# Second slots of a mixture-of-experts layer: units of two experts by half the sequences, in one block with the first slots

## The reference, cut to what matters

```python
GROUP = 64; E1, S1, E2 = (8, 16, 4)
logits1 = einsum('bGgd,esd->bGges', xg, phi)
disp1 = softmax(logits1, axis=2)
comb1 = softmax(logits1.reshape(b, G, g, E1 * S1), -1)
slots = einsum('bGgd,bGges->bGesd', xg, disp1)            # first slots
yn = _l2norm(slots) * scale * gamma2
means = yn.reshape(b, G, E1, m, ns, d).mean(axis=4)       # m = 4 means per expert
se2 = einsum('bGkmd,kdf->bGkmf', means, w_slot2)          # second slots
se2 = _l2norm(se2.reshape(..., E2, d)...) * scale
logits2 = einsum('bGksd,bGkemd->bGksem', yn, se2)
disp2 = softmax(logits2, axis=3)
comb2 = softmax(logits2 ..., -1)
slots2 = einsum('bGksd,bGksem->bGkemd', yn, disp2)        # dispatch: inputs of the experts
u = einsum('bGkemd,kedh->bGkemh', slots2, w1) + b1        # 32 small experts
...
```

## Time and profile before

| what | value |
|---|---|
| median of 3 runs | 555.93 us |
| lowest, highest | 555.88, 558.68 us |
| profiled execution, whole time | 558.41 us |
| its span, first to last instruction | 556.6 us |
| mean granted clock of TensorE | 0.997 |
| PE busy | 529.9 us (95%) |
| DVE busy | 314.0 us (56%) |
| ACT busy | 251.7 us (45%) |
| POOL busy | 103.1 us (19%) |

### The profile page before, as it was taken

One profiled execution on the slowest core, in us unless ns is written; L12 is line 12 of the kernel. 1 busy time (PEld: TensorE's weight loads), 2 busy tenths in 40 slices (PEclk: granted clock), 3 DMA queues, 4 the chain that ended last, 5 costly groups with the idle time before them and its releaser, 6 DMA issues. The chain is left out here.

```text
span 556.6 us, 13660 instructions
## 1 busy us (share of the span) xinstructions
PE 529.9 (95%) x5485; PEld 438.6 (79%) x5485; DVE 314.0 (56%) x727; ACT 251.7 (45%) x807; POOL 103.1 (19%) x189
## 2 busy tenths in 40 slices
PE   6999999999999999999898999999989999999996
PEld 5888888865566566666777856988879999999985
DVE  2348679666877776663268745376634444444433
ACT  1234343456656656644377558456732222222210
POOL 6380000011044034321217700000100000000000
PEclk9999999999999999999999999999999999999998
DMA  6090000000000000000380032000059999999643
GB/s 242 16 317 3 2 0 2 1 1 1 1 2 2 2 1 1 1 2 1 112 358 2 2 126 88 2 1 2 1 194 409 276 347 369 363 309 332 164 58 114
DMA packets 20724, 58.82 MB, mean 106 GB/s; under 512 B 3043, under 2 KB 9797, under 8 KB 20549
## 3 DMA queue, kind: packets, MB, share of 16 engines
q1 hardware_dynamic: 14756, 49.47, 24.8%
q0 software_dynamic: 1056, 4.33, 4.1%
q10 hardware_dynamic: 4848, 4.13, 2.7%
HBM read 53.21 MB, written 4.33 MB: 103 GB/s over the span
## 5 line engine op out<-in xcount | busy, mean ns | idle before, releaser
L2030 PE MATMUL banks<-slots_t,w 64*128 64x128 f32 x1344 | 80.7, 272 | 1.1 <-PEq L1654 1.1
L1135 DVE TENSOR_REDUCE qk<-banks 128x4 f32<-128x1024 f32 x48 | 58.8, 1225 | 39.5 <-PE banks L598 39.5
L2030 PEld LDWEIGHTS banks<-slots_t,w 64*128 64x128 f32 x1344 | 79.1, 188 | 1.5 <-issue 1.3
L598 PE MATMUL banks<-qk_t 16*128 16x256 f32 x384 | 54.4, 400 | 2.6 <-DVE qk L1135 2.4
L605 PE MATMUL banks<-qk_t 17*128 17x256 f32 x384 | 54.4, 400 | 0.0
L598 PEld LDWEIGHTS banks<-qk_t 16*128 16x128 f32 x384 | 33.2, 184 | 20.3 <-issue 13.8
L2133 DVE TENSOR_REDUCE tokens<-banks 128x192 f32<-128x384 f32 x32 | 17.8, 557 | 47.3 <-PE banks L2061 47.3
L99 PE MATMUL banks<-ident 128*128 128x128 f32 x342 | 43.4, 278 | 0.0
L99 PEld LDWEIGHTS banks<-ident 128*128 128x128 f32 x342 | 40.3, 192 | 2.7 <-issue 2.6
L914 ACT ACTIVATE wk_t<-banks 128x512 f32<-128x512 f32 x48 | 26.1, 595 | 32.8 <-PE banks L605 32.8
L338 POOL TENSOR_TENSOR qk<-qk,att_rms 128x384 f32<-128x384 f32 x14 | 11.4, 837 | 150.6 <-ACT att_rms L886 150.6
(11 more groups left out here) (243 smaller groups left out, 1114.8 us busy)
## 6 DMA issues: line engine op xcount, KB each, us to landing
w<-in_w SPq DMA_DIRECT2D x28, 768.0 KB, 11.9
w<-in_w2e SPq DMA_DIRECT2D x24, 384.0 KB, 12.4
w_slot<-in_w_slot SPq DMA_DIRECT2D x8, 576.0 KB, 4.2
yn_t<-in_w SPq DMA_DIRECT2D x4, 768.0 KB, 11.0
yn_t<-in_w2e SPq DMA_DIRECT2D x8, 384.0 KB, 14.1
rows_scratch<-tokens ACTq DMA_DIRECT2D x28, 96.0 KB, 7.1
yn_all<-rows_scratch POOLq DMA_DIRECT2D x7, 384.0 KB, 9.5
out<-h SPq DMA_DIRECT2D x8, 192.0 KB, 1.9
```

What stands on the lines that cost most here:

```text
L598: last_best = nc.tensor.matmul(g.ps[MAXES[hh]][:, half * SEQ:(half + 1) * SEQ], g.qk_t[bn_ % 2][row:row + HDIM, bq, 0, half * P:(half + 1) ...
L1135: nc.vector.tensor_reduce(to, flat(MAXES[0], MAXES[1] + 1).rearrange("p (h t n) -> p h t n", h=2, n=SEQ), AX.X, ALU.max, negate=True).then ...
L2030: return nc.tensor.matmul(bank[:, j * P:(j + 1) * P], g.w1[n % BUFS][rows, first + j * P:first + (j + 1) * P], x, start=start, stop=stop, ...
```

## The change

The two functions become one, `slots_and_dispatch`, with one block. Its parts:

1. The second slots are made in eight units `u` instead of eight experts. A unit is two experts for half the sequences (16 groups, 64 columns of means). Units 0 to 3 are for sequences 0 to 3, units 4 to 7 for sequences 4 to 7. `make_se2(u)` has eight matmuls in place of four: each is 64 columns wide and goes to the lower or upper 64 partitions of a bank. `parts` yields four copies each for DVE and ACT, of half the size, in place of two.
2. `make_se2(0)` stands ahead of the last `make_slots`, where twelve `keep_busy` matmuls stood. `make_se2(1)` follows `turn_last`. The DVE list has `norm_se2(0)` and `norm_se2(1)` among the seven `sum_last` reductions, and on ACT `keep_last` follows the third unit.
3. The logits of sequence 0 and their softmax stand among the last two units. Of the 87 `keep_busy` matmuls in the two functions 23 are left: 3 at the start as before, 16 before `turn_last`, 4 in the last sequence.
4. In the dispatch `make_weights` is split in two, with `turn_disp` between the halves.
5. All eight weight tiles are loaded at the start of the block: three in `w_slot2`, four in the tiles of `w1`, one in the region that later holds `slots2_t`, which also holds the temporaries of the first slots. `w1` of the first four experts is loaded when all units are made.
6. Since two blocks with their semaphores stand where three were, the mixer's 53 semaphores (`early_semaphore`) are cleared by SP at the end of the mixer's own block, after the last projection, and no longer in the next block.

```diff
@@ mixer_and_attention, SP
+            sp.wait_ge(S["projected"], BATCH)
+            sp.wait_ge(S["mixed_kept"], BATCH)
+            sp.wait_ge(S["divided"], BATCH)
+            sp.wait_ge(S["tokens_made"], BATCH - 2)
+            g.clear_early(sp)
@@ slots_and_dispatch
+        weights2 = [*g.w_slot2, *(tile[:, 0:3 * E2 * DIM // 2] for tile in g.w1), carve([P, 3 * E2 * DIM // 2])]
+        MADE = (2, 4, 2, 4, 0, 2, 4, 0)
@@ PE: a unit
+                for b in range(2):
+                    for x in range(2):
+                        nc.tensor.matmul(g.ps[MADE[u] + b][x * REST:(x + 1) * REST, 0:COLS], means(x, slice(0, P), 0),
+                                         weights2[first + x][:, b * COLS:(b + 1) * COLS], start=True, stop=False,
+                                         skip_group_check=True)
+                for x in range(2):
+                    for b in range(2):
+                        rows = slice(b * REST, (b + 1) * REST)
+                        last = nc.tensor.matmul(g.ps[MADE[u] + b][x * REST:(x + 1) * REST, 0:COLS], means(x, rows, 1),
+                                                weights2[first + x][rows, 2 * COLS:3 * COLS], start=False, stop=True,
+                                                skip_group_check=True)
@@ PE: its list from the last pass of first slots on
-            pe.wait_ge(S["comb_kept"], BATCH - 1)
-            keep_busy(nc, g, 2, 12)
+            make_se2(0)
             make_slots(BATCH - 1)
             turn_yn(BATCH - 2)
             turn_comb(BATCH - 1)
-            keep_busy(nc, g, 2, 12)
+            pe.wait_ge(F["rest_kept"], BATCH - 2)
+            keep_busy(nc, g, 1, 16)
             turn_last(BATCH - 1)
-            keep_busy(nc, g, 2, 18)
+            make_se2(1)
+            for u in range(2, UNITS):
+                make_se2(u)
+                turn_se2(u - 2)
+            make_logits(0)
+            turn_se2(UNITS - 2)
+            turn_logits(0)
+            turn_se2(UNITS - 1)
+            for n in range(1, BATCH):
+                make_logits(n)
+                make_weights(n - 1, range(0, PAIRS))
+                turn_disp(n - 1)
+                make_weights(n - 1, range(PAIRS, GPS))
+                turn_logits(n)
+                make_inputs(n - 1)
@@ ACT
+            for u in range(UNITS):
+                root_se2(u)
+                if u >= 2:
+                    keep_se2(u - 2)
+                if u == 2:
+                    keep_last(BATCH - 1)
+            row_exp(0)
+            keep_se2(UNITS - 2)
+            col_exp(0)
+            keep_se2(UNITS - 1)
@@ DVE
             norm_slots(BATCH - 1)
-            sum_last(BATCH - 1)
+            norm_se2(0)
+            sum_last(BATCH - 1, slice(0, 4))
+            norm_se2(1)
+            sum_last(BATCH - 1, slice(4, 7))
+            keep_se2(0)
+            for u in range(2, UNITS - 1):
+                norm_se2(u)
+                keep_se2(u - 1)
+            mask(0)
+            norm_se2(UNITS - 1)
+            keep_se2(UNITS - 2)
+            col_max(0)
+            invert_row(0)
+            keep_se2(UNITS - 1)
+            dispatch(0)
@@ SP
+            for k in range(E1):
+                sp.dma_start(weights2[k][:, :], g.d["w_slot2"][k]).then_inc(weights2_loaded[k // 2], 16)
+            for n in range(EARLY):
+                load_output(sp, g, n)
+            g.clear_before(sp)
+            sp.wait_ge(S["made"], UNITS)
+            for n in range(EARLY):
+                load_hidden(sp, g, n)
...
```

More of the change, by code:

```diff
@@ L7 @@
+import math
 from contextlib import ExitStack
@@ new lines, in logits @@
+            def logits(n):
+                pe.wait_ge(F["kept"], n + 1)
+                if n >= 2:
+                    pe.wait_ge(F["comb_exped"], TPS * (n - 1))
+                    pe.wait_ge(F["comb_kept"], n - 1)
+                if n >= 3:
+                    pe.wait_ge(F["rest_kept"], n - 2)
+                for part in range(2):
+                    for to_slots in (True, False):
+                        for t in range(TPS):
+                            rows, c = chunks(t)[part]
+                            of_x, of_phi = x_t[n % 2][rows, c, :], g.phi_t[rows, c, :]
+                            lhs, rhs = (of_phi, of_x) if to_slots else (of_x, of_phi)
+                            first = 0 if to_slots else P
+                            last = nc.tensor.matmul(g.ps[FIRST_LOGITS(n)[t]][:, first:first + P], lhs, rhs,
+                                                    start=(part == 0 and to_slots), stop=(part == 1),
+                                                    skip_group_check=True)
+                last.then_inc(F["logits"], 1)
@@ new lines, in make_slots @@
+            def make_slots(n):
+                pe.wait_ge(F["disp_kept"], n + 1)
+                if n:
+                    pe.wait_ge(F["slots_normed"], GPS * n)
+                for t in range(TPS):
+                    for half in range(2):
+                        rows = slice(GROUP * half, GROUP * (half + 1))
+                        last = nc.tensor.matmul(g.ps[SLOTS[half]][:, AND_ONE(t)], disp[n % 2][rows, t, :],
+                                                x[n][rows, AND_ONE(t)], start=True, stop=True)
+                last.then_inc(F["slots_made"], 1)
@@ L1803, in _ @@
-            make_weights(BATCH - 1)
+            turn(0)
+            keep_busy(nc, g, 6, 3)
+            turn(1)
+            for n in range(BATCH):
+                logits(n)
+                if n + 2 < BATCH:
+                    turn(n + 2)
+                if n:
+                    make_slots(n - 1)
+                    turn_comb(n - 1)
+                if n >= 2:
+                    turn_yn(n - 2)
+                turn_first_disp(n)
+            make_se2(0)
+            make_slots(BATCH - 1)
@@ L1881, in norm, with norm_se2 @@
+            def norm_se2(k):
                 dve.wait_ge(S["rooted"], k + 1)
```

709 lines of the change are left out of this document (333 added, 376 removed).

## The result

The changed kernel takes 541.88 us (median of 4 runs, 540.96 to 544.31) against 556.62 us of the kernel before (median of 4, 555.88 to 558.68). The ratio is 0.9736, with a 95% interval from 0.9694 to 0.9779: 14.7 us faster. The prediction was 542.5 us, range 539.5 to 549.5. The profiled execution took 544.31 us (span 542.5), the highest of the four.

A forecast was written before the change was run, and what follows sets the result against it. PE was taken as the bound, with idle multiplications and a dispatch hole to win. Gains of 11.8 and 2.8 less 1.1 us gave 13.5 off the 555.93 median: 542.4, rounded to 542.5 us, range 539.5 to 549.5.

The forecast's parts named there:

- the part up to `make_logits(2)`: From the old idle multiplications at 311.23 us through the units: `make_logits(2)` starts at 354.8 instead of 366.64, 11.8 us earlier.
- the dispatch: Half of the weights covers PE's 0.40 us hole before `make_inputs`: 2.4 us over six sequences plus 0.4 in the tail, 2.8.
- the mixer's end: SP's 53 clears ahead of the mixer's block end move it and everything after by 1.1 us, bounds 0 and 1.5.
- Price of a unit: PE's products for one unit: first part 1.45 us, second 0.85, together 2.30; 3.23 with transposes.
- The rival with 0.13: Array quarters don't overlap in a unit's second part, which takes 1.70 us: total 548.7 us, chance 0.13.
- the slower one: Halves don't overlap in a unit's first part: a unit takes 4.6 us, total 561 us, chance 0.04.
- as an expert was: A unit's 2.30 us of products on PE equals that of one expert in the kernel before.
- the drain: TensorE drains on a change of tiling mode, 0.12 us at most; one more per unit means 1.0 us less gain.
- To the last slots: With `make_se2(0)` ahead, the last slots start 0.1 us later and `turn_last` 1.1 later than before.
- The waits in the units: PE's waits among units and at the seam: 0.1, 0.35, 0.55 (unit 6) and 2.2 (unit 7), together 3.2 us.
- The clock: Rival: PE's clock falls in the 2.2 us wait or after the mixer's end, costing 1.7 us: 544.2 us, chance 0.07.
- PE is dense before it: Argument against the clock rival: PE works densely before the 2.2 us wait, which is also shorter than the earlier case's 2.65.

The follow-up runs named there:

- seam experiment: Kernel with early clears, plus ACT copying unit 6 before sequence 0's row exponentials and DVE scaling unit 7 before masking sequence 0: median 538.49 us, ratio 0.9685.
- unit 0 late: Changed kernel with unit 0 moved behind `turn_last` and the 12 idle multiplications back in its place: median 547.04 us.
- early clears: Changed kernel with the four waits ahead of SP's 53 semaphore clears one sequence lower: median 541.69 us, five runs from 539.31 to 542.29.
- shorter cover: Kernel with early clears, with 11 idle multiplications before `turn_last` in place of 16: 539.22 and 539.51 us at clock 1.0, others 540.19 to 542.41.

## Why the prediction was right

The distance without falls moved by 13.3 us; the sum was 13.5. Of its terms, the part up to `make_logits(2)` brought 12.07 us without the fall (11.8 forecast), the dispatch 2.69 (2.8), and the mixer's end cost 1.45 (1.1). Runs at a mean clock of 1.0 agree: 541.8 us after and 555.4 before, 13.6 less. The 14.7 us between the two medians hold about a microsecond that is not the change's.

- *Price of a unit.* 2.30 us was forecast and 2.25 measured; with transposes 3.27 (327.75 to 331.02) against 3.23. The open question, four quarters or pairs, came out as four: 0.81 us, where pairs would be 1.70. The rival with 0.13 is excluded, and the slower one too, since the first part takes 1.44. The rule of the Trainium skill ("TensorEngine Tiling (Array Packing)", "Tiling Modes") that 64x64 is four independent tiles agrees with this trace. But "as an expert was" holds only against the first expert, from which the price was read. A later one takes 3.16 us with its transposes (334.73 to 337.89), so a unit is 0.11 longer, nearly all of it in the transposes (1.0 from their start to the next unit, 0.93 before).

```profile
334.73 1.46 PE L1708 MATMUL banks<-w_slot,means_t 128*128 128x384 f32 x4
```

  That is the size of the drain that the prediction bounded at 0.12 us. The Trainium skill says that a change of the tiling mode drains TensorE ("TensorEngine Tiling (Array Packing)", "Key Properties"); the extra 0.11 us would fit that, but no run here isolates it.
- *To the last slots.* They start 3.23 us behind the last `turn_disp`, where it was 3.05; 0.1 later was forecast, 0.18 measured. `turn_last` starts 1.07 us later behind the last `turn_disp` (8.59 for 7.52), 1.1 forecast. Unit 0 in the place of the idle multiplications was worth 3.0 us.
- *The waits in the units.* I had 0.1 and 0.35 at units 1 and 2; the trace has none. At unit 6 it is 0.35 (forecast 0.55), at unit 7 2.35 (forecast 2.2). The last was read from ACT's order, and the seam experiment agrees. ACT's four copies take 0.89 us where I had taken 1.1, which may be why the early waits did not come; no run tests it.
- *The dispatch.* 2.69 us against 2.8, and 3.0 by the experiment that undoes it.
- *The mixer's block end.* Mis-sized: 1.1 us forecast, 1.45 measured, within the bounds of 0 to 1.5. A clear takes longer than the 0.062 us read from before. SP waits until about 269.2 and is done at about 272.9, near 0.07 each. The experts' block agrees (last load ahead of its 57 clears, next load):

```profile
401.43 0.43 SPq L1311 DMA_DIRECT2D w<-in_w2e  x1
405.65 0.33 SPq L1306 DMA_DIRECT2D w<-in_w  x1
```

  That is 3.79 us from the end of the one to the start of the other, 0.066 for each of 57. As forecast, this one costs nothing, the tile being needed seven experts later.
- *The clock.* Here the weighing was poor. I gave the fall 0.07 as one case among others, at 1.7 us. It came in 2 of 10 runs of the changed kernel, each time at both places that I had named, and cost 3.0 us together. "PE is dense before it" was no protection. The Trainium skill ("TensorE: Matmul & The Clock Gate", Part 1) has 1.2 GHz for an idle PE; the trace agrees, with a granted clock of 0.50 at 276 us. How often it would come, nothing that I had could say.
- *The two values of the runs.* I took 555.9 and 558.7 as two values of unknown cause. The clock explains a part: of the later runs of the kernel before those at 1.0 lie at 553.9 to 557.3, those at 0.997 at 556.3 to 558.3, one at 0.994 at 560.0, so the groups overlap. The profile of before had one fall, at its end, 1.7 us, which the change doesn't touch. That the profiled executions came out as forecast too (544.31 for 544.9) is luck: two falls of 3.0 us together in the one stand against a fall of 1.7, a wait longer by 1.0 and a start later by 1.2 us in the other.

So the number was right by its steps. The block's end cost 0.35 us more than forecast and the early units waited 0.45 less; that these two cancelled is luck.

## What to carry to other kernels

Idle work that is there to keep an engine's clock up counts as busy, so look for it first: independent work that fits its length is nearly free there, and the second engine of the chain starts sooner too (one unit of 2.25 us was worth 3.0). Work that looks like housekeeping, such as clears of semaphores on the queue of DMAs, has a price of 0.06 to 0.07 us apiece and becomes the bound if it stands behind the last event before a barrier. When two pipelines are joined, write down for each engine what stands ahead of the operation that the other pipeline waits for: exchanging two neighbours on ACT and two on DVE won 0.9 us of a wait of 2.35. Before reading a difference of a microsecond, put the granted clock of each run beside its time, and compare a distance inside the traces that leaves out the loads at the start and the end.

## What the runs showed that was not expected

- A pause of 1.75 us on PE was followed by half clock in three profiles: both of the changed kernel and that of the kernel with unit 0 late. It was not in the kernel before with the clears added, nor in the kernel with the weights undivided, whose pause is 1.75 us too and which is the changed kernel instruction for instruction up to there. The two stretches from 268 to 280 us, changed kernel and then undivided weights, with the granted clock third from the end:

```profile
268.00:280.00 12.00, 8.85 (x61) 7.85 (x60) 2.18 (x7) 3.01 (x12) 2.99 (x3) 0.86 0.49 179
```

```profile
268.00:280.00 12.00, 8.84 (x71) 7.88 (x69) 2.67 (x9) 3.55 (x14) 3.13 (x4) 1.00 0.44 153
```

  So neither the pause's length nor the program decides it; what does is open. The wait of 2.35 us before the last unit's transposes is the same: a fall behind it in four profiles, none in three.
- Taking a pause away (early clears) didn't make falls rarer: three of five runs are at 0.997, against 2 of 10 of the changed kernel below 0.999. With so few runs this may be chance, and where these three fell is not known.
- Falls are not of one length: 1.4 to 1.6 us in the first slots and at the last unit of the changed kernel, but 2.95 us in the kernel with the shorter cover (from the last unit's transposes to the experts 49.56 us, against 46.61 without it), where the clock was 0.75 from 345 to 350 us and 0.57 from 350 to 355. The work behind the wait is the same in both.
